# A graph network's first sweep over its edges: six one-hot columns in one VectorE instruction instead of two at a time

## The chip, the cores and the metric

The kernel runs on one core of a Trainium2 chip. The metric is the device time of one execution in microseconds, lower is better. Engines are named as the profile names them: PE (TensorE), DVE (VectorE), ACT (ScalarE), POOL (GpSimd), SP (SyncE).

## The reference

Four graph layers follow one another on 3125 nodes with 128 features, each with a residual and a layer normalisation. There are 103,125 directed edges `src -> dst`, sorted by `dst`, with a weight each. Layer 0 is dot-product attention over the edges, then a small dense network. Layer 1 has two convolutions that sum weighed neighbours. Layer 2 is three attention passes of another kind, and layer 3 a normalised convolution. Cut to what this change touches:

```
# layer 0
Q, K, V = x @ Wq + bq, x @ Wk + bk, x @ Wv + bv          # (3125, 8 heads, 16)
scores = sum(Q[dst] * K[src], -1) / sqrt(16)             # per edge and head
alpha = softmax of scores over the edges of one dst
out = segment_sum(alpha * V[src], dst) @ Wo + bo
# layers 1 and 3
agg = segment_sum(x[src] * edge_weight[:, None], dst)    # = A @ x, A[dst, src] = summed weights
```

## The kernel before

The edges are cut into steps of 128. Four steps make a group, and there are 208 groups. A function `dot_scores_and_adjacency` (L1055 on) sweeps once over all edges and does two jobs at a time, for which five engines run programs of their own, tied by counting semaphores. The loop body holds 8 groups (a ring turn, `RING_GROUPS`) and runs 26 times.

The first job is the scores of layer 0. For each step POOL gathers 128 rows of keys and values from memory into `rows` (L810, four gathers a group, one step each). ACT makes a one-hot matrix `hot_t` of the destinations from a row of local numbers (L1125 squares, L1127 clamps). PE multiplies it with the three bfloat16 parts of the queries (L1235, 12 matmuls a group, "the query matmuls"). DVE multiplies the result in PSUM by the gathered keys (`z`, L1207) and sums over each head (`logits`, L1210).

The second job builds the dense weighed adjacency matrix for layers 1 and 3, which later passes read. The edges are cut once more, into steps sorted for this job, 6 a group (`A_GROUP`). For each step DVE makes two one-hot matrices, `at_hot` (128 edges x 200, where in a span of windows the edge falls, L1183) and `lo_hot` (128 x 128, the source's low bits, L1187), and multiplies the latter by the edge weights (L1193). PE multiplies the two (L1250, with a small clearing matmul at L1247 for each pair of steps; "the adjacency matmuls"). ACT copies finished parts of PSUM to `stage` (L1166), and SP stores them in memory, a block at a time (L1107).

What sets the order around the change:

- In its loop DVE calls `make_adjacency_hots(n + 2)`, waits for the query matmuls (`asked`) and the gathered rows of group n (`landed`), and does z and logits of group n. `lo_hot` and `at_hot` have four slots (`A_HOTS`), so hots n+2 wait for the adjacency matmuls of group n-2 (`summed`).
- DVE raises `hots` behind L1187 and `weighed` behind L1193, once for each group, on the last instruction of the run. L1193 works in place and waits for `hots`.
- PE's program for group n waits for `hot_made` n, and for the logits of group n-2 (`zed`), whose PSUM bank it takes. Then come the 12 query matmuls, the waits for `hots` and `weighed` of group n, and the adjacency matmuls. In front of every second group its sequencer reads two small tables from SBUF into registers (L1227 and L797).
- ACT's program for group n begins, in every second group, with a table read (L1149) and the ask for the rows of groups n+4 and n+5 (`index_ring`, L1119), which waits for the logits of group n-3. It makes `hot_t` n+1, copies the adjacency parts of group n, waits for the rows of group n and stores their values half.
- POOL gathers as soon as the index of a pair of groups is there and the ring's place is free.

Of the kernel before, what the change touches and what calls it, by code (L numbers as in the profile page):

```python
# [22 lines left out]
ALU = mybir.AluOpType  # L23
# [4 lines left out]
P = 128  # L28
# [34 lines left out]
SPAN = BLOCKS * WIN  # L63
A_GROUP = 6
# [105 lines left out]
def over_groups(t):  # L170
    return t.rearrange("p (k d) -> p k d", d=D)
# [883 lines left out]
def dot_scores_and_adjacency(B, A, table, heads, query_parts, logits, loads):  # L1055
# [6 lines left out]
    with ExitStack() as ctx:  # L1062
# [5 lines left out]
        lo = B.sb(ctx, "lo_hot", [P, A_HOTS, A_GROUP, P])  # L1068
        at = B.sb(ctx, "at_hot", [P, A_HOTS, A_GROUP, SPAN])
# [5 lines left out]
        hots, weighed, summed, copied, room, stored = (  # L1075
            B.count("adj_" + n) for n in ("hots", "weighed", "summed", "copied", "room", "stored"))
        wait_holder = B.count("wait_holder")

        def group_rows(q, lo_col):
            return rows[:, q * GROUP * width:(q + 1) * GROUP * width].rearrange(  # L1080
                "p (k w) -> p k w", w=width)[:, :, lo_col:lo_col + D]

        def steps_of(t, n, k):
            return t[:, bass.ds(n * A_GROUP + k, 2)].rearrange("p (k o) -> p k o", o=1)

        with nc.Block() as block:
            @block.gpsimd
            def _(eng):
                with eng.Fori(0, RING_TURNS) as i:
                    for h in range(RING_GROUPS // 2):  # L1090
                        eng.wait_ge(index.sem, index.at(h + 1) + i * (RING_GROUPS // 2))
                        for q in range(2 * h, 2 * h + 2):
                            eng.wait_ge(kept[q].sem, kept[q].at(0) + i * 16)
                            eng.sem_inc(wait_holder.sem, 1)
                            for s in range(q * GROUP, (q + 1) * GROUP):
                                gather_rows(B, eng, rows, table, width, s, landed)
# [79 lines left out]
            @block.vector  # L1176
            def _(eng):
                eng.sem_inc(zed.sem, RING_GROUPS * 2)

                def make_adjacency_hots(n, slot):  # L1180
                    eng.wait_ge(summed.sem, summed.at(A_PAIRS) + n * A_PAIRS)
                    for k in range(0, A_GROUP, 2):
                        eng.tensor_tensor(at[:, slot, k:k + 2, :],  # L1183
                                          A.iota[:, :].rearrange("p (o n) -> p o n", o=1).to_broadcast([P, 2, SPAN]),
                                          steps_of(A.at, n, k).to_broadcast([P, 2, SPAN]), ALU.is_equal)
                    for k in range(0, A_GROUP, 2):
                        ins = eng.tensor_tensor(lo[:, slot, k:k + 2, :],  # L1187
                                                B.iota[:, :].rearrange("p (o n) -> p o n", o=1).to_broadcast([P, 2, P]),
                                                steps_of(A.lo, n, k).to_broadcast([P, 2, P]), ALU.is_equal)
                    ins.then_inc(hots.sem, 1)  # L1190
                    eng.wait_ge(hots.sem, hots.at(1) + n)
                    for k in range(0, A_GROUP, 2):
                        ins = eng.tensor_tensor(lo[:, slot, k:k + 2, :], lo[:, slot, k:k + 2, :],  # L1193
                                                steps_of(A.w, n, k).to_broadcast([P, 2, P]), ALU.mult)
                    ins.then_inc(weighed.sem, 1)

                for n in range(2):
                    make_adjacency_hots(n, n)
                with eng.Fori(0, RING_TURNS) as i:
                    for q in range(RING_GROUPS):  # L1200
                        n = i * RING_GROUPS + q
                        make_adjacency_hots(n + 2, (q + 2) % A_HOTS)
                        eng.wait_ge(asked.sem, asked.at(3) + n)
                        for s in range(q * GROUP, (q + 1) * GROUP):
                            eng.wait_ge(landed[s].sem, landed[s].at(16) + i * 16)
                        zz = z[:, q % 2, :]
                        eng.tensor_tensor(over_groups(zz), over_groups(B.bank(q % 2)), group_rows(q, 0), ALU.mult  # L1207
                                          ).then_inc(zed.sem, 1)
                        eng.wait_ge(zed.sem, zed.at(RING_GROUPS * 2 + 1) + n * 2)
                        eng.tensor_reduce(logits[:, bass.ds(n * (GROUP * heads), GROUP * heads)],  # L1210
                                          zz.rearrange("p (m d) -> p m d", d=dim), X_AXIS, ALU.add).then_inc(zed.sem, 1)
# [1729 lines left out]
```

## Time and the profile before

| | |
|---|---|
| median of three runs | 6320.31 us |
| the runs | 6324.8, 6320.31, 6304.53 us |
| profiled execution: time and span | 6324.8 us, 6322.7 us |
| busy share of the span: PE, DVE, ACT, POOL | 71%, 74%, 43%, 58% |
| mean granted clock of TensorE | 0.724 |
| the stage that holds the change | about 272 to 1480 us |

The profile is one execution. Times are microseconds unless marked ns. A group of instructions is a line with its engine, operation and tiles; its row gives the count, busy time, the mean of one, and the idle time of the engine just in front of them with what ended it. "Issue" is idle time that no semaphore in the profile explains. DVEq, ACTq and PEldq are the engines' sequencers. PEld is the loading of weights, which overlaps PE.

### The profile page before, as it was taken

The page shows a single profiled execution, that of the slowest core. Times are in us where ns is not written, and L with a number is a line of the kernel's source. Part 1 is how long each engine was busy: PE and PEld are TensorE (multiplying, and loading weights), DVE is VectorE, ACT ScalarE, POOL GpSimd, SP SyncE. Part 2 cuts the span into 40 slices and gives each one's busy share as a digit, 9 for nine tenths or more (in the row PEclk, how much of TensorE's full clock was granted, in tenths as well). Part 3 has the DMA queues.
Part 4 walks back from the last instruction along what each step waited for, and adds up shares of the span by engine and source line. Part 5 has one row for each costly group of instructions (what it writes and reads, how often), then busy time and mean ns, then how long its engine had stood idle before and what let it go on. Part 6 is the DMA issues. An engine that isn't in the chain of part 4 may idle for free. (4 is left out here: it accounts for less than half of the span.)

```text
span 6322.7 us, 128259 instructions
## 1 busy us (share of the span) xinstructions
PE 4480.2 (71%) x25366; PEld 3482.7 (55%) x25375; DVE 4705.6 (74%) x10133; ACT 2709.9 (43%) x6587; POOL 3669.3 (58%) x3881
## 2 busy tenths in 40 slices
PE   0578887884888896777777747777776577777746
PEld 0466666663666454556655636555555456665523
DVE  3788888887766415888888788888886988888843
ACT  0244554453554201455555525555455344554530
POOL 1476776671332001777777657777774777777710
PEclk9988888886999998565565656565656565666668
DMA  1376676674443573333333223333231233322225
GB/s 49 95 201 185 189 199 189 188 197 93 129 133 121 161 267 120 88 90 86 84 89 90 59 75 88 81 89 90 80 89 51 76 83 84 81 78 83 73 94 179
DMA packets 577604, 723.40 MB, mean 114 GB/s; under 512 B 89995, under 2 KB 424673, under 8 KB 576927
## 3 DMA queue, kind: packets, MB, share of 16 engines
q1 hardware_dynamic: 305030, 352.76, 18.4%
q0 software_dynamic: 123968, 277.70, 16.2%
q10 hardware_dynamic: 148056, 86.42, 5.1%
q8 instruction: 247, 4.05, 0.3%
q14 instruction: 303, 2.47, 0.1%
HBM read 595.96 MB, written 120.58 MB: 113 GB/s over the span
## 5 line engine op out<-in xcount | busy, mean ns | idle before, releaser
L1629 POOL DMA_INDIRECT rows<-scratch_gat,index x2496 | 2553.1, 1023 | 1324.7 <-issue 744.9
L2007 PE MATMUL sums<-mix,vhot 128*128 128x128 f32 x4992 | 1112.1, 392 | 3.1 <-issue 0.3
L810 POOL DMA_INDIRECT rows<-scratch_kv,index_ring x832 | 847.8, 1019 | 397.4 <-issue 238.0
L1952 PE MATMUL sums<-xr_part,hot_t 128*128 x7524 | 999.3, 286 | 93.0 <-DVE hot_t L1768 64.7
L2007 PEld LDWEIGHTS sums<-mix,vhot 128*128 128x128 f32 x4992 | 951.6, 284 | 50.9 <-issue 2.3
L1952 PEld LDWEIGHTS sums<-xr_part,hot_t 128*128 128x128 bf16 x7524 | 775.1, 126 | 281.1 <-issue 126.9
L1696 ACT ACTIVATE moved_sums<-sums x624 | 372.5, 597 | 1212.5 <-PE sums L2007 1104.8
L1686 ACT ACTIVATE vhot<-iota,edge_local 128x128 f32<-128x128 f32 x2496 | 789.1, 390 | 0.0
L1250 PE MATMUL sums<-at_hot,lo_hot 128*128 128x200 f32 x2496 | 668.8, 423 | 2.6
L1868 DVE TENSOR_TENSOR z<-sums,rows 128x512 f32<-128x512 f32 x624 | 426.7, 684 | 251.7 <-DMA rows<-scratch_gat,index 214.1
L1250 PEld LDWEIGHTS sums<-at_hot,lo_hot 128*128 128x128 f32 x2496 | 510.7, 236 | 61.2 <-issue 28.0
L2003 PE MATMUL sums<-zeros 128*128 128x8 bf16 x624 | 115.2, 185 | 569.4 <-ACT vhot L1690 311.6
L1854 DVE TENSOR_TENSOR mix<-rows,alpha 128x512 f32<-128x512 f32 x624 | 432.5, 694 | 69.4 <-PE sums L2007 18.9
L1876 DVE TENSOR_TENSOR z<-z,gat_a 128x512 f32<-128x512 f32 x624 | 432.7, 693 | 48.3 <-DVE carry L1813 4.3
L1690 ACT ACTIVATE vhot<-vhot,part 128x512 f32<-128x512 f32 x624 | 450.4, 722 | 20.3
L1235 PE MATMUL sums<-q_part,hot_t 128*128 x2496 | 321.9, 238 | 185.1 <-issue 125.9
L1870 DVE SCALAR_TENSOR_TENSOR z<-z 128x512 f32<-128x512 f32 x624 | 432.8, 694 | 21.5
L2003 PEld LDWEIGHTS sums<-zeros 128*128 128x128 bf16 x624 | 64.2, 103 | 698.2 <-issue 697.9
L1878 DVE TENSOR_REDUCE logits<-z 128x16 f32<-128x512 f32 (+1 forms) x624 | 428.7, 687 | 21.2
L1235 PEld LDWEIGHTS sums<-q_part,hot_t 128*128 128x128 bf16 x2496 | 227.1, 105 | 303.0 <-issue 255.3
L1166 ACT ACTIVATE stage<-sums x624 | 298.4, 498 | 171.0 <-PE sums L1250 146.3
L1183 DVE TENSOR_TENSOR at_hot<-adj_iota,adj_at 128x400 f32<-128x400 f32 x630 | 323.6, 568 | 6.5 <-PEq L1216 6.5
(510 smaller groups left out, 6585.1 us busy)
## 6 DMA issues: line engine op xcount, KB each, us to landing
piece<-scratch_adj SPq DMA_DIRECT2D x90, 1280.0 KB, 6.0
local_ring<-scratch_local_rows SPq DMA_DIRECT2D x633, 128.0 KB
scratch_spool<-rows ACTq DMA_DIRECT2D x208, 256.0 KB, 3.2
vals<-scratch_spool SPq DMA_DIRECT2D x208, 256.0 KB, 2.6
scratch_adj<-stage SPq DMA_DIRECT2D x25, 1600.0 KB
rows<-scratch_gat,index POOLq DMA_INDIRECT x2496, 2.5
local_ring<-scratch_local_rows ACTq DMA_DIRECT2D x211, 128.0 KB
mask<-scratch_masks SPq DMA_DIRECT2D x234, 80.1 KB
```

The source lines that it names most:

```text
L810: eng.indirect_dma_start(slots[:, s * width:(s + 1) * width], None, table, bass.IndirectOffsetOnAxis(ap=B.index_ring[:, s:s + 1], axis=0)) ...
L1235: ins = eng.matmul(B.ps[:, (q % 2) * 512 + k * D:(q % 2) * 512 + (k + 1) * D], hot_t[:, q % 2, k * P:(k + 1) * P], part[:, bass.ds(at_bloc ...
L1250: ins = eng.matmul(B.ps[:, bass.ds(here, SPAN)], lo[:, q % A_HOTS, k, :], at[:, q % A_HOTS, k, :], start=False, stop=True, skip_group_chec ...
L1629: eng.indirect_dma_start(rows[:, slot, q, k * D:(k + 1) * D], None, table, bass.IndirectOffsetOnAxis(ap=index[:, slot, s:s + 1], axis=0)). ...
L1686: ins = eng.activation(hot[:, v % MIXES, k * P:(k + 1) * P], B.iota[:, :], ACT.Square, scale=-1.0, bias=B.edge_local[:, bass.ds(m * GROUP ...
L1690: eng.activation(hot[:, v % MIXES, :], hot[:, v % MIXES, :], ACT.Relu, bias=B.part[:, 2:3], scale=-4.0).then_inc(hot_v.sem, 1)
L1854: eng.tensor_tensor(mix[:, v % MIXES, :].rearrange("p (k h d) -> p k h d", k=GROUP, h=heads), rows[:, of, v, :].rearrange("p (k h d) -> p ...
L1870: eng.scalar_tensor_tensor(out=zz, in0=zz, scalar=SLOPE, in1=zz, op0=ALU.mult, op1=ALU.max).then_inc(reduced.sem, 1)
L1876: eng.tensor_tensor(over_groups(zz), over_groups(zz), a, ALU.mult).then_inc(reduced.sem, 1)
L1878: eng.tensor_reduce(in_portion(lg[:, slot, 0:R], q), zz.rearrange("p (k h d) -> p k h d", k=GROUP, h=heads), X_AXIS, ALU.add).then_inc(red ...
L1952: ins = eng.matmul(B.ps[:, at + k * D:at + (k + 1) * D], hot_t[:, slot, k * P:(k + 1) * P], part[:, bass.ds(at_block, D)], start=(j == 0), ...
L2007: ins = eng.matmul(B.ps[:, bass.ds(of_block * D, D)], hot[:, v % MIXES, k * P:(k + 1) * P], mix[:, v % MIXES, k * D:(k + 1) * D], start=Fa ...
```

## The change

In `make_adjacency_hots`, each of three loops over three pairs of steps becomes one instruction over all six steps of the group. L1183 made 2 x 200 elements a partition and is now one of 6 x 200; L1187 and L1193 made 2 x 128 and are now 6 x 128. The operands are the same tensors with the same broadcasts, the semaphores are raised at the same points of the sequence, and all other programs stay as they are.

```diff
-        def steps_of(t, n, k):
-            return t[:, bass.ds(n * A_GROUP + k, 2)].rearrange("p (k o) -> p k o", o=1)
+        def steps_of(t, n):
+            return t[:, bass.ds(n * A_GROUP, A_GROUP)].rearrange("p (k o) -> p k o", o=1)
...
                 def make_adjacency_hots(n, slot):
                     eng.wait_ge(summed.sem, summed.at(A_PAIRS) + n * A_PAIRS)
-                    for k in range(0, A_GROUP, 2):
-                        eng.tensor_tensor(at[:, slot, k:k + 2, :],
-                                          A.iota[:, :].rearrange("p (o n) -> p o n", o=1).to_broadcast([P, 2, SPAN]),
-                                          steps_of(A.at, n, k).to_broadcast([P, 2, SPAN]), ALU.is_equal)
-                    for k in range(0, A_GROUP, 2):
-                        ins = eng.tensor_tensor(lo[:, slot, k:k + 2, :],
-                                                B.iota[:, :].rearrange("p (o n) -> p o n", o=1).to_broadcast([P, 2, P]),
-                                                steps_of(A.lo, n, k).to_broadcast([P, 2, P]), ALU.is_equal)
-                    ins.then_inc(hots.sem, 1)
+                    eng.tensor_tensor(at[:, slot, :, :],
+                                      A.iota[:, :].rearrange("p (o n) -> p o n", o=1).to_broadcast([P, A_GROUP, SPAN]),
+                                      steps_of(A.at, n).to_broadcast([P, A_GROUP, SPAN]), ALU.is_equal)
+                    eng.tensor_tensor(lo[:, slot, :, :],
+                                      B.iota[:, :].rearrange("p (o n) -> p o n", o=1).to_broadcast([P, A_GROUP, P]),
+                                      steps_of(A.lo, n).to_broadcast([P, A_GROUP, P]), ALU.is_equal).then_inc(hots.sem, 1)
                     eng.wait_ge(hots.sem, hots.at(1) + n)
-                    for k in range(0, A_GROUP, 2):
-                        ins = eng.tensor_tensor(lo[:, slot, k:k + 2, :], lo[:, slot, k:k + 2, :],
-                                                steps_of(A.w, n, k).to_broadcast([P, 2, P]), ALU.mult)
-                    ins.then_inc(weighed.sem, 1)
+                    eng.tensor_tensor(lo[:, slot, :, :], lo[:, slot, :, :],
+                                      steps_of(A.w, n).to_broadcast([P, A_GROUP, P]), ALU.mult).then_inc(weighed.sem, 1)
```

## Rows read from the trace of the kernel before

**Rows 1.** The page, busy time, share of the span and instructions of each engine.

```profile
PE 4480.2 (71%) x25366; PEld 3482.7 (55%) x25375; DVE 4705.6 (74%) x10133; ACT 2709.9 (43%) x6587; POOL 3669.3 (58%) x3881
```

**Rows 2.** Busy time in one stretch, the stage with the changed lines.

```profile
core 0: us, PE busy (x) PEld busy (x) DVE busy (x) ACT busy (x) POOL busy (x), PEclk, DMA share, GB/s
272.00:1480.00 1208.00, 991.81 (x5604) 794.02 (x5605) 1026.50 (x2291) 604.39 (x1140) 844.32 (x829) 0.83 0.68 190
```

**Rows 3.** DVE's groups in the stage: count, busy, mean ns, idle before.

```profile
L1183 DVE TENSOR_TENSOR at_hot<-adj_iota,adj_at 128x400 f32<-128x400 f32 x624 | 320.5, 568 | 0.0
L1193 DVE TENSOR_TENSOR lo_hot<-lo_hot,adj_w 128x256 f32<-128x256 f32 x627 | 232.5, 424 | 25.5
L1187 DVE TENSOR_TENSOR lo_hot<-iota,adj_lo 128x256 f32<-128x256 f32 x624 | 225.9, 416 | 0.0
L1207 DVE TENSOR_TENSOR z<-sums,rows 128x512 f32<-128x512 f32 x208 | 143.1, 688 | 126.2 <-PE sums L1235 116.8 <-DMA rows<-scratch_kv,index_ring 4.4 <-issue 3.4
L1210 DVE TENSOR_REDUCE logits<-z 128x512 f32 x208 | 142.7, 686 | 29.7
```

**Rows 4.** PE's groups in the stage.

```profile
L1250 PE MATMUL sums<-at_hot,lo_hot 128*128 128x200 f32 x2491 | 667.9, 423 | 2.6
L1235 PE MATMUL sums<-q_part,hot_t 128*128 x2490 | 321.0, 238 | 183.2 <-issue 125.9 <-ACT hot_t L1127 52.8 <-DVE z L1207 2.0
L1247 PE MATMUL sums<-zeros 128*128 128x8 bf16 x623 | 114.3, 183 | 30.3 <-issue 24.3 <-DVE lo_hot L1193 5.5 <-ACT stage L1166 0.2
```

**Rows 5.** POOL's group in the stage.

```profile
L810 POOL DMA_INDIRECT rows<-scratch_kv,index_ring x829 | 844.3, 1018 | 346.2 <-issue 237.4 <-ACT index_ring L1119 108.8
```

**Rows 6.** Who waited for whom in the stage: us in total, times, longest.

```profile
PE sums L1235 <- issue: 125.9, 66, 5.4
DVE z L1207 <- PE sums L1235: 116.8, 111, 4.9
PE sums L1235 <- ACT hot_t L1127: 52.8, 57, 1.6
ACT index_ring L1119 <- DVE z L1207: 45.0, 19, 3.6
```

**Rows 7.** PE's table reads in the stage: ns, least, median, most.

```profile
L1227 PEldq TENSOR_LOAD <-adj_pe_table x103: 764/1094/3308, 279.6 to 1468.6; - x103
...
L797 PEldq TENSOR_LOAD <-blocks x103: 528/544/2348, 281.0 to 1469.5; - x103
```

**Rows 8.** Timeline of DVE around 800 us: start, length.

```profile
794.07 0.69 DVE L1210 TENSOR_REDUCE logits<-z 128x512 f32 x1
...
800.23 0.69 DVE L1210 TENSOR_REDUCE logits<-z 128x512 f32 x1
800.83 1.53 DVE L1183 TENSOR_TENSOR at_hot<-adj_iota,adj_at 128x400 f32<-128x400 f32 x3
802.28 1.09 DVE L1187 TENSOR_TENSOR lo_hot<-iota,adj_lo 128x256 f32<-128x256 f32 x3
803.49 1.10 DVE L1193 TENSOR_TENSOR lo_hot<-lo_hot,adj_w 128x256 f32<-128x256 f32 x3
...
805.33 0.69 DVE L1210 TENSOR_REDUCE logits<-z 128x512 f32 x1
```

**Rows 9.** Timeline of PE in the same stretch.

```profile
802.63 1.80 PE L1235 MATMUL sums<-q_part,hot_t 128*128 x12 [0.81 <-issue]
804.65 0.18 PE L1247 MATMUL sums<-zeros 128*128 128x8 bf16 x1 [0.23 <-DVE lo_hot L1193]
```

**Rows 10.** Timeline of POOL in the same stretch.

```profile
801.41 1.28 POOL L810 DMA_INDIRECT rows<-scratch_kv,index_ring  x1 [0.30 <-issue]
803.00 1.19 POOL L810 DMA_INDIRECT rows<-scratch_kv,index_ring  x1 [0.30 <-issue]
804.49 0.94 POOL L810 DMA_INDIRECT rows<-scratch_kv,index_ring  x1 [0.30 <-issue]
```

**Rows 11.** Gathers by source line: ns, least, median, most; the stage, then the later stages.

```profile
L810 POOL DMA_INDIRECT rows<-scratch_kv,index_ring x829: 940/947/1366, 272.0 to 1461.3; - x166
...
L1629 POOL DMA_INDIRECT rows<-scratch_gat,index x2496: 940/944/1461, 2489.6 to 5992.8; - x192
```

## The prediction

> **What bounds the kernel now.** I read the page first: over the whole span DVE is the busiest engine and PE is next [rows 1]. That is an average over stages, so I then asked where the changed lines run. Lines L1183, L1187 and L1193 occur in one stage alone, from about 272 to 1480 us, and the summary of that stretch is the first thing to see: 1208 us, in which DVE is busy for 1026 us, PE for 992 and POOL for 844 [rows 2]. The stage has 208 groups, so a group takes 1208 / 208 = 5.81 us. DVE looks like the bound, at 85%. Three views say otherwise.
>
> The groups of instructions by line close the time of each engine. For DVE: 4.94 us busy a group, 0.61 us idle in front of z (126.2 us), nearly all of it ended by PE's query matmuls, and the rest semaphore gaps [rows 3]. For PE: 4.77 us busy and 213.5 us idle in front of L1235 and L1247, 1.03 us a group; together 5.80 us, the whole group [rows 4]. What ends PE's idle time is "issue" (125.9 us) and ACT's hot_t (52.8 us); DVE is named for 2.0 + 5.5 us in the whole stage [rows 4, 6]. The issue time is PE's own sequencer: once every two groups it reads two tables, with medians of 1.09 and 0.54 us, before it can issue the next query matmuls [rows 7]. So the chain that sets the pace is PE with its table reads, and at times ACT. The granted clock of this stage is 0.83, a mix of the 2.4 and the 1.2 GHz level [rows 2]; the change doesn't touch PE's work.
>
> Third, does PE ever wait for what DVE makes? The code lets DVE build hots for group n+2 in front of z of group n, and PE's query of group n needs the logits of group n-2. In the timeline the query at 802.63 could use logits made by the reduction of 794.07, over 7 us earlier, and the adjacency matmuls at 804.65 read hots finished two DVE rounds before [rows 8, 9]. The releaser "DVE lo_hot" beside the latter is the round for group n+2 that merely happened to end then. The same holds for ACT's ask, put down to z for 45.0 us [rows 6]: its semaphore value is that of the reduction of group n-3, and what delays it is its own table read.
>
> **The change, part by part.** *Fewer instructions.* Nine become three in each group. Two rows of the same form give DVE's rate: 568 ns for 400 elements and 416 ns for 256 [rows 3], 1.06 ns an element and about 0.15 us fixed. But back to back they overlap: three L1183 take 1.53 us, not 1.70, so they start (1.53 - 0.568) / 2 = 0.48 us apart, three L1187 start (1.09 - 0.416) / 2 = 0.34 us apart [rows 8]. These starts differ by 0.14 us for 144 elements, near 1 ns each, and taking 1.04 ns leaves 0.48 - 0.42 = 0.06 and 0.34 - 0.27 = 0.07 us that each instruction of a run pays besides. Six are removed: 6 x 0.07 = 0.42 us a group. From below, the saving could be nothing if six repeats streamed slower (no row shows six; with two, L1187's 416 ns are no more than L1193's 424 for as many elements); from above it is the whole fixed part, 6 x 0.15 = 0.9 us. I take 0.42, because the rows back to back are this very sequence. The new instructions should last 0.568 + 800 x 1.06 = 1.41, 0.416 + 512 x 1.06 = 0.96 and 0.42 + 0.54 = 0.96 us. Over 208 groups DVE has 87 us less to do.
>
> What is that worth? DVE's round takes 5.10 us when it waits for nothing (800.23 to 805.33) and will take 4.68 [rows 8]. The group takes 5.81 by PE. Where DVE already waits for the query, it waits 0.42 us longer: nothing. Where it runs late after a long PE step (PE's steps alternate, as the table reads fall in every second), z starts earlier, and its product is used only two or three groups later, so nothing again. The value is 0 from this side. Should the cover be gone, the price is the second rival below.
>
> *The order of signals.* hots and weighed were raised only by the third instruction of each run and now by the only one; no wait is added. At the start, hots 0 to 2 come 3 x 0.42 = 1.3 us earlier, but z of group 0 waits for its rows as well; I count 0 to 1 us gained. The last groups end in PE's matmuls and ACT's copies, so the end gains nothing.
>
> *POOL.* This is the part that may cost. The view of POOL's gathers by source line shows 940 ns at the least, 947 in the median, 1366 at the most [rows 11], with a mean of 1018 [rows 5]. The timeline tells which are stretched: the gather of 801.41 began inside the run of L1183 and took 1.28 us, that of 803.00 inside L1187's and took 1.19, that of 804.49 inside L1193's and took 0.94 [rows 8, 10]. The excess, 0.34 us in the first case, is the time to the end of the single DVE instruction that was running, and the most (1366 - 944 = 0.42 us) is about one 400-element step. In the later stages, where DVE's instructions beside the gathers have 512 elements, the most is 1461, an excess of 0.52 us [rows 11]. So the excess grows with the length of the one instruction, and it will reach 1.41 and 0.96 us where it was 0.42 and 0.3.
>
> Cost of it: a gather and the gap behind it take 0.944 + 0.30 = 1.25 us [rows 10], as long as the merged L1183 blocks, so about one gather in each group begins in it and waits 0 to 1.3 us, 0.65 in the mean; the next one then begins beyond L1187's end mostly. Now the excess is (1018 - 944) x 4 = 0.30 us a group. POOL's group goes from 4 x 1.25 + 0.30 = 5.28 to 4.98 + 0.65 = 5.63 us, at worst 4.98 + 1.3 = 6.3. POOL has 108.8 us of waits for its index in the stage, 0.52 us a group [rows 5], so 0.35 more is covered, and by the code the ask runs four groups ahead of z. At the chosen value this edit costs nothing; only over 0.8 us of excess a group, 5.81 - 4.98, does it set the pace.
>
> The Trainium skill ("SBUF — State Buffer", section "SBUF: two separate sides") states that a Vector instruction with two SBUF inputs holds a port pair that it shares with GpSimd for its whole length, so that the other waits fully. By this rule, the trace agrees for L1183 and L1187 but not for L1193, which has two SBUF inputs too and stretches no gather in the rows shown. If the merged L1193 did block, a gather would meet it with a chance of 0.96 / 1.25 and wait 0.48 us in the mean, 0.37 us more a group, and the excess would be 0.65 + 0.37 = 1.02 us instead of 0.65; that is the second price of the first rival.
>
> **Sum.** 0 (DVE's saving is covered) - 1 (start) + 0 (POOL covered) = -1 us on an execution of 6324.8 us with a span of 6322.7. That execution is the slowest of three, whose median is 6320.3; on the median the forecast is 6320 us.
>
> **Rivals.** *POOL becomes the bound (slower).* For it: only 0.17 us of cover is left by my mean (0.52 - 0.35), and in stretches such as that of 800 us a group takes 5.1 us, not 5.81 [rows 8]. Against it: the gathers have a lead to spend before z misses its rows, and z waited for rows only 4.4 us [rows 3]. If each group waits the full 1.3 us, it is (6.28 - 5.81) x 208 = +98 us, 6418; if the excess is 1.0 us a group, (5.98 - 5.81) x 208 = +35 us, 6355. It decides from 0.8 us a group.
>
> *DVE is the bound after all (faster).* For it: 85% busy, and DVE waited for PE before z in 111 of 208 groups [rows 6], so in 97 it came last. If each of those gives its 0.42 us to the end, -41 us, 6279; if all 208 do, -87 us, 6233. Against it: PE waits for no product of DVE beyond 7.5 us in all. The Trainium skill ("VectorE: DVE Perf Modes", section on the TRN2 errata) says that a fixed latency is paid by each instruction, given as 58 cycles at 0.96 GHz, and advises tiles of 512 elements or more. Estimated by that page it would be 6 x 208 x 60 ns = 75 us, if DVE set the pace.
>
> *Shifted transfers, either sign.* PE's table reads range from 0.76 to 3.3 us [rows 7]. The gathers will start at other moments, and if the mean read moved by 0.1 us, 104 pairs of groups would move the end by 10 us, inside what I call no change.
>
> **From this to the numbers.** A time within 0.3% (19 us) is about what a measurement of this kernel can't tell from none; the three runs shown spread by 0.32%. My forecast has 0.58, with 6300 to 6340 as its own range; POOL as the bound 0.20; DVE as the bound 0.15; transfers shifted beyond 0.3% 0.07, split evenly but for a little more on the faster side. So faster 0.19, same 0.58, slower 0.23. The range reaches to the partial price of each rival: 6279 below, and 6370 above, between the 35 and the 98 us.
>
> **What the changed profile would show.** The three lines 208 to 210 times each at 1.41, 0.96 and 0.96 us; DVE busy some 80 us less in the stage and its idle time in front of z, ended by PE, some 80 us more; PE's idle time in front of L1235 the same, with the same releasers; gathers of the stage up to 2.2 us at the most with a mean of 1.08 to 1.12, and POOL's waits for the index down from 109 us to some 40. The stage would still end near 1480 us. The prediction is wrong if the waits of z for gathered rows rise over some 20 us (POOL), if the idle time of PE shrinks (DVE was on the path), or if gathers stretch under the merged L1193 too, a third blocking window of 0.96 us.

## The result: slower by 1.3%, and the profile after

The changed kernel takes 6403.15 us in the median of 4 runs (6393.4 to 6404.46), against 6322.56 us before. The ratio is 1.0131 with a 95% interval of 1.0108 to 1.0152. The forecast of 6320 us was wrong, and the time lies above the range: the first rival, POOL as the bound, which had a chance of 0.20 and prices of 6355 and 6418 us, is what happened.

The summary of the stage that holds the change, by the same columns as [rows 2]; the stage now ends some 80 us later:

```profile
272.00:1560.00 1288.00, 1055.64 (x5602) 829.80 (x5601) 932.12 (x1034) 599.92 (x1138) 1036.01 (x828) 0.81 0.64 178
```

A group takes 1288 / 208 = 6.19 us instead of 5.81. DVE has 94 us less to do, POOL is busy 192 us more. The groups by line, from 272 to 1480 us, answer to [rows 3 to 5]; in the same time fewer groups are done, 194 instead of 208:

```profile
L1182 DVE TENSOR_TENSOR at_hot<-adj_iota,adj_at 128x1200 f32<-128x1200 f32 x195 | 273.2, 1401 | 1.6 <-issue 0.4
L1189 DVE TENSOR_TENSOR lo_hot<-lo_hot,adj_w 128x768 f32<-128x768 f32 x194 | 185.9, 958 | 23.9
L1185 DVE TENSOR_TENSOR lo_hot<-iota,adj_lo 128x768 f32<-128x768 f32 x194 | 184.6, 952 | 0.0
L1202 DVE TENSOR_TENSOR z<-sums,rows 128x512 f32<-128x512 f32 x194 | 133.8, 690 | 280.4 <-DMA rows<-scratch_kv,index_ring 256.4 <-PE sums L1230 23.6
```

```profile
L1230 PE MATMUL sums<-q_part,hot_t 128*128 x2334 | 323.7, 242 | 180.6 <-issue 83.8 <-ACT hot_t L1127 59.3 <-DVE logits L1205 17.8
```

```profile
L810 POOL DMA_INDIRECT rows<-scratch_kv,index_ring x778 | 972.7, 1250 | 237.1 <-issue 233.7 <-ACT index_ring L1119 3.4
```

DVE's new instructions last what was forecast, 1401, 952 and 958 ns. But z now waits 256 us for gathered rows, where it waited 4.4, and POOL hardly waits for its index any more (3.4 us, it was 108.8): POOL has become the engine that sets the pace. Its gathers last 1250 ns in the mean, not 1018, so four take 4 x (1.25 + 0.30) = 6.2 us, the length of a group. POOL's lead is gone as well: matched by their order, a z of the kernel before starts 16.3 us after the end of the last gather that it needs, in the median, and 2.8 us after it in the changed kernel. The view by source line gives the extremes, to be read beside [rows 11]:

```profile
L810 POOL DMA_INDIRECT rows<-scratch_kv,index_ring x832: 941/1004/2184, 267.6 to 1561.9; - x167
```

The timelines of DVE and of POOL over one round show where the time goes:

```profile
801.81 1.40 DVE L1182 TENSOR_TENSOR at_hot<-adj_iota,adj_at 128x1200 f32<-128x1200 f32 x1
803.12 0.95 DVE L1185 TENSOR_TENSOR lo_hot<-iota,adj_lo 128x768 f32<-128x768 f32 x1
804.20 0.96 DVE L1189 TENSOR_TENSOR lo_hot<-lo_hot,adj_w 128x768 f32<-128x768 f32 x1
806.76 0.69 DVE L1202 TENSOR_TENSOR z<-sums,rows 128x512 f32<-128x512 f32 x1 [1.60 <-DMA rows<-scratch_kv,index_ring]
807.59 0.69 DVE L1205 TENSOR_REDUCE logits<-z 128x512 f32 x1
808.19 1.40 DVE L1182 TENSOR_TENSOR at_hot<-adj_iota,adj_at 128x1200 f32<-128x1200 f32 x1
```

```profile
802.84 1.19 POOL L810 DMA_INDIRECT rows<-scratch_kv,index_ring  x1 [0.30 <-issue]
804.33 1.65 POOL L810 DMA_INDIRECT rows<-scratch_kv,index_ring  x1 [0.30 <-issue]
806.28 0.95 POOL L810 DMA_INDIRECT rows<-scratch_kv,index_ring  x1 [0.30 <-issue]
807.53 0.95 POOL L810 DMA_INDIRECT rows<-scratch_kv,index_ring  x1 [0.30 <-issue]
808.78 1.63 POOL L810 DMA_INDIRECT rows<-scratch_kv,index_ring  x1 [0.30 <-issue]
```

The gather of 802.84 began inside the merged L1182 (to 803.21) and took 0.24 us longer than a free one. The next began at 804.33, 0.13 us into the merged multiplication, and took 0.70 us longer. The one that began in z's wait and the one that began between z and the reduction took 0.95 us. The rule that fits all of them: a gather that begins inside a DVE instruction with two SBUF inputs is held until 0.12 us before that instruction's end. And the position is no accident: a gather released at the end of L1182 is followed by the next 1.25 us later, just inside L1189 (0.13 to 0.14 us after its start in every round). Counted over the records from 272 to 1480 us, 197 gathers began in L1182 and took 0.51 us longer in the mean, and 194, one in each round, began in L1189 and took 0.70 us longer. Three of the 197 were not held at all: they began within 0.03 us after the start of L1182.

### The profile page after: what moved, and what is told of

Its sections match the earlier page's. It is cut to its first block and busy times, and to the rows that moved or that the text cites. A ratio compares the mean times of both kernels' runs of the same rounds, so it can differ in the third digit from the quotient of the medians.

```text
span 6401.5 us, 125759 instructions
## 1 busy us (share of the span) xinstructions
PE 4549.2 (71%) x25374; PEld 3522.9 (55%) x25375; DVE 4617.8 (72%) x8873; ACT 2707.0 (42%) x6587; POOL 3869.9 (60%) x3881
## 5 line engine op out<-in xcount | busy, mean ns | idle before, releaser
L810 POOL DMA_INDIRECT rows<-scratch_kv,index_ring x832 | 1042.5, 1253 | 304.1 <-issue 249.9
L1245 PE MATMUL sums<-at_hot,lo_hot 128*128 128x200 f32 x2496 | 696.6, 436 | 4.4
L1863 DVE TENSOR_TENSOR z<-sums,rows 128x512 f32<-128x512 f32 x624 | 427.6, 685 | 263.6 <-DMA rows<-scratch_gat,index 218.0
L1245 PEld LDWEIGHTS sums<-at_hot,lo_hot 128*128 128x128 f32 x2496 | 530.1, 243 | 68.1 <-issue 32.2
L1230 PE MATMUL sums<-q_part,hot_t 128*128 x2496 | 346.6, 242 | 193.3 <-issue 88.6
L1202 DVE TENSOR_TENSOR z<-sums,rows 128x512 f32<-128x512 f32 x208 | 143.5, 690 | 303.1 <-DMA rows<-scratch_kv,index_ring 278.2
```

Of the source, the lines that this page charges most:

```text
L810: eng.indirect_dma_start(slots[:, s * width:(s + 1) * width], None, table, bass.IndirectOffsetOnAxis(ap=B.index_ring[:, s:s + 1], axis=0)) ...
L1230: ins = eng.matmul(B.ps[:, (q % 2) * 512 + k * D:(q % 2) * 512 + (k + 1) * D], hot_t[:, q % 2, k * P:(k + 1) * P], part[:, bass.ds(at_bloc ...
L1245: ins = eng.matmul(B.ps[:, bass.ds(here, SPAN)], lo[:, q % A_HOTS, k, :], at[:, q % A_HOTS, k, :], start=False, stop=True, skip_group_chec ...
```

## Experiments

The phase theory: POOL's gathers lock to DVE's round. What a gather costs is set by which instruction it meets, and that by the order and lengths of the instructions. Four gathers need 5.7 us of a round in the changed kernel, by hand: held in L1182, released at 1.27, at 2.53 held in L1189 to 3.2, then 4.48 and 5.73. These 5.7 us are too few, and by them alone the gathers would fit into the 5.81 us of a group: POOL took 4.98 + 1.23 = 6.2 us, as the count begins at the release in L1182 and leaves out the 0.5 us for which the gather is held there. The other times by hand in the expectations below are too low as well (with the swapped order 4.7 us, against 4.98 + 0.62 = 5.6); it is the measured excess that is compared. A first rival says that a merged instruction costs by its length, wherever it stands; a second says that the longer DVE instructions hurt PE or ACT and not POOL.

**One run merged, or two.** Each of these differs from the changed kernel in the loops alone. `{c}` is 2 (as before) or 6 (merged):

```diff
+                    for k in range(0, A_GROUP, {c}):
+                        eng.tensor_tensor(at[:, slot, k:k + {c}, :], ... steps_of(A.at, n, k, {c}) ..., ALU.is_equal)
+                    for k in range(0, A_GROUP, {c}):
+                        ins = eng.tensor_tensor(lo[:, slot, k:k + {c}, :], ... steps_of(A.lo, n, k, {c}) ..., ALU.is_equal)
...
+                    for k in range(0, A_GROUP, {c}):
+                        ins = eng.tensor_tensor(lo[:, slot, k:k + {c}, :], lo[:, slot, k:k + {c}, :], ..., ALU.mult)
```

Only `at_hot` merged: 

> Only at_hot merged. Phase theory: behind the gather held in at, the next begins at 2.53 us, at the start of the first short multiplication, held 0 or 0.3 us; four fit in 5.0 to 5.3 us; 6310 to 6335 us. Rival by length: half of the loss, 6362. Rival DVE: 6340 or more.

Only `lo_hot` merged: 

> Only lo_hot merged, once more, on a chip where the kernel before takes its usual time. Phase theory: gathers at 1.70 (held 0.59 us in the merged lo), 3.54 and 4.79; four fit in 4.8 us; 6310 to 6325 us. Rival by length: a quarter of the loss, 6342.

Only the multiplication merged: 

> Only the multiplication merged. Phase theory: gathers come at 1.70, 3.00 (held 0.49 us in the merged multiplication) and 4.75, then 6.0; four fit in 4.8 to 6.0 us by where the first begins; 6315 to 6345 us, and in the trace gathers that begin inside L1193's successor are held to 0.12 us before its end, although none was before. Rival by length: a quarter of the loss, 6342. If this line blocked nothing at any length, no gather would be held in it and the time would be 6320 or less.

`at_hot` and `lo_hot` merged, the multiplication in three: 

> at_hot and lo_hot merged, the multiplication by the weights left in three instructions. Phase theory: the gather behind the one held in at begins 2.53 us into the round, 0.14 us into the first of three short multiplications, and is held 0.16 us instead of 0.70; four gathers fit in 5.2 us instead of 5.7; 6320 to 6345 us. Rival by length (loss of 80 us shared by the squares of 1.40, 0.95 and 0.96 us): three quarters stay, 6380. Rival DVE: between, 6370 to 6400.

Measured, with the gather's mean of the stage (272 to 1470 us) and the excess it makes over 944 ns, four times a group:

| merged | time, us | ratio (95%) | gather mean, ns | excess a group, us | z waits for rows, us |
|---|---|---|---|---|---|
| none (before) | 6322 | 1 | 1018 | 0.30 | 4.4 |
| multiplication | 6331.25 | 1.0014 (0.9998 to 1.003) | 1065 | 0.48 | 10.3 |
| lo | 6324.8 | 1.0012 (1.0002 to 1.0021) | 1070 | 0.50 | 11.4 |
| at | 6332.84 | 1.0022 (1.0007 to 1.0036) | 1084 | 0.56 | 13.8 |
| at, lo | 6332.1 | 1.0021 (1.0005 to 1.0038) | 1167 | 0.89 | 110.9 |
| all | 6403.15 | 1.0131 (1.0108 to 1.0152) | 1251 | 1.23 | 253.9 |

No single run costs more than 0.22%, and the three together cost far more than the sum (0.5%). The rival by length forecast 6342 to 6380 us for these and falls. The column of z's waits tells where POOL's room ends: 4 to 14 us up to an excess of 0.56 us, 111 at 0.89 and 254 at 1.23. The time does not follow as closely: the multiplication alone and `at_hot` alone, with 0.48 and 0.56 us, were 10 and 11 us slower, as much as the kernel with 0.89. With the multiplication split, the gather behind the one held in L1183 still begins just inside it, but is held for one short instruction only. In that kernel's timelines of DVE and POOL the excess is 0.17 us where it was 0.70:

```profile
804.90 1.10 DVE L1193 TENSOR_TENSOR lo_hot<-lo_hot,adj_w 128x256 f32<-128x256 f32 x3
```

```profile
805.03 1.11 POOL L810 DMA_INDIRECT rows<-scratch_kv,index_ring  x1 [0.30 <-issue]
```

The kernel with only the multiplication merged shows that this line holds gathers, too; here one began 0.33 us into it and took 0.50 us longer:

```profile
807.66 0.96 DVE L1193 TENSOR_TENSOR lo_hot<-lo_hot,adj_w 128x768 f32<-128x768 f32 x1
```

```profile
807.99 1.44 POOL L810 DMA_INDIRECT rows<-scratch_kv,index_ring  x1 [0.30 <-issue]
```

**All merged, in another order.** The same three instructions, with `lo_hot` built first:

```diff
+                    eng.tensor_tensor(lo[:, slot, :, :], ..., ALU.is_equal).then_inc(hots.sem, 1)
                     eng.tensor_tensor(at[:, slot, :, :], ..., ALU.is_equal)
-                    eng.tensor_tensor(lo[:, slot, :, :], ..., ALU.is_equal).then_inc(hots.sem, 1)
                     eng.wait_ge(hots.sem, hots.at(1) + n)
```

> All three runs merged as in the changed kernel, with lo_hot built in front of at_hot. Phase theory (a gather that begins inside a DVE instruction with two SBUF inputs is held to about 0.12 us before its end, and the next begins 1.25 us later, so the order of the instructions decides what it meets): held in lo, a gather is released at 0.83 us of the round, the next begins at 2.08 near the end of at (0.87 to 2.19), the next at 3.4 beside z, the fourth at 4.7. Four gathers fit in a round of 4.7 us, against 5.7 us in the changed kernel; the loss goes: 6320 us, within 20. Rival by length (each merged instruction costs by its length, whatever its place): 6400, as changed. Rival DVE (longer DVE instructions hurt PE and ACT directly, not POOL): 6400.

Measured 6323.16 us, ratio 1.0001 (0.9988 to 1.0014): the whole loss is gone with every instruction as long as before the swap. The gather's mean is 1100 ns, an excess of 0.62 us a group. The timelines of DVE and POOL show the phases as forecast. Held in lo, the gather is released, the next begins near the end of at, and the one after that beside z:

```profile
803.36 0.95 DVE L1183 TENSOR_TENSOR lo_hot<-iota,adj_lo 128x768 f32<-128x768 f32 x1
804.23 1.40 DVE L1188 TENSOR_TENSOR at_hot<-adj_iota,adj_at 128x1200 f32<-128x1200 f32 x1
805.55 0.95 DVE L1193 TENSOR_TENSOR lo_hot<-lo_hot,adj_w 128x768 f32<-128x768 f32 x1
807.04 0.69 DVE L1207 TENSOR_TENSOR z<-sums,rows 128x512 f32<-128x512 f32 x1 [0.54 <-PE sums L1235]
```

```profile
803.43 1.70 POOL L810 DMA_INDIRECT rows<-scratch_kv,index_ring  x1 [0.30 <-issue]
805.43 1.01 POOL L810 DMA_INDIRECT rows<-scratch_kv,index_ring  x1 [0.30 <-issue]
806.75 0.95 POOL L810 DMA_INDIRECT rows<-scratch_kv,index_ring  x1 [0.30 <-issue]
808.00 0.94 POOL L810 DMA_INDIRECT rows<-scratch_kv,index_ring  x1 [0.30 <-issue]
```

It also prices DVE's saving: with POOL inside its room (z waits 14.2 us for rows and 231.6 us for PE), some 87 us less work on DVE are worth nothing.

**Half of the gathers.** Two kernels, the one before and the changed one, gather for every second step only, so the scores of the others are not computed; POOL clears the tile first (6.9 us). The waits of ACT and DVE for these rows go with them.

```diff
+                eng.memset(rows[:, :], 0.0).then_inc(cleared.sem, 1)
...
-                            for s in range(q * GROUP, (q + 1) * GROUP):
+                            for s in range(q * GROUP, (q + 1) * GROUP, 2):
                                 gather_rows(B, eng, rows, table, width, s, landed)
```

> The kernel before with every second gather of this stage left out, once more, beside a kernel before whose time is that of the first runs. PE theory: PE's chain with its table reads sets the pace, so the time stays within 30 us of the kernel before, plus some 8 us for the clearing of the tile at the start. Rival: if gathers or their traffic paced the stage before, 50 us less or more.

> The changed kernel with every second gather of this stage left out, once more. Phase theory: POOL needs only two gathers a round, the holds cost nothing, and the time is that of the run beside it within 10 us. Rival DVE (the longer DVE instructions hurt PE or ACT directly): it lies 80 us above the run beside it.

Measured 6304.88 us (ratio 0.9972, 0.9956 to 0.9987) and 6306.21 us (0.9982, 0.9965 to 0.9998). The second lies 1.3 us above the first, as expected: the changed kernel loses nothing when POOL has room, although its gathers are held more than ever (1346 ns in the mean, against 1029). Leaving out half of the gathers gains 14 to 18 us in the kernel before (by the medians and by the ratio), within the 30 us expected, and 7 more with the clearing counted; so the gathers were not the bound there, but not quite free either. The rival that the longer instructions hurt PE or ACT falls.

**Short instructions with one tensor.** One tensor-scalar instruction for each step, the weight applied in the same instruction (where `hots` and `weighed` are raised is cut here):

```diff
+                    for k in range(A_GROUP):
+                        eng.tensor_scalar(at[:, slot, k, :], A.iota[:, :], A.at[:, bass.ds(n * A_GROUP + k, 1)], None, ALU.is_equal)
+                    for k in range(A_GROUP):
+                        ins = eng.tensor_scalar(lo[:, slot, k, :], B.iota[:, :], A.lo[:, bass.ds(n * A_GROUP + k, 1)],
+                                                A.w[:, bass.ds(n * A_GROUP + k, 1)], ALU.is_equal, ALU.mult)
...
```

> Tensor-scalar instructions, one for each step, once more. Phase theory: holds of at most one short instruction, a gather's mean near 0.95 us. If the loop of PE and ACT sets the pace, no gain although DVE and POOL both have more room: 6320 within 20. Rival (DVE or POOL sets it): 6280 or less.

Measured 6337.59 us, ratio 1.0018 (1.0002 to 1.0035). POOL's row shows the excess nearly gone, a mean of 953 ns, and 183 us of waits for the index:

```profile
L810 POOL DMA_INDIRECT rows<-scratch_kv,index_ring x823 | 784.3, 953 | 414.7 <-issue 231.4 <-ACT index_ring L1119 183.2
```

DVE (906 us busy up to 1480 us, 1026 before) and POOL both have more room and the time does not fall: neither was the bound before. The holds are short rather than absent, and the single tensor does not keep them away. This gather began 0.10 us into the second of the `at_hot` instructions, which start 0.23 us apart and last some 0.32 us each, and it took 0.10 us longer:

```profile
294.54 1.48 DVE L1183 TENSOR_SCALAR at_hot<-adj_iota,adj_at 128x200 f32<-128x200 f32 x6
```

```profile
294.87 1.04 POOL L810 DMA_INDIRECT rows<-scratch_kv,index_ring  x1 [0.30 <-issue]
```

In the stage 210 gathers began in an `at_hot` instruction; 49 of them were held by more than 0.03 us, 0.15 us at the most, and again to some 0.12 us before its end. Under `lo_hot`, with two scalars, it was 5 of 297.

**PE's table read moved.** The block numbers of the next pair of groups are read between the query and the adjacency matmuls of the odd group, in the kernel before and in the changed one:

```diff
+                        if q % 2 == 1:
+                            blocks.read((q + 1) % RING_GROUPS, 2, n + 1)
                         eng.wait_ge(hots.sem, hots.at(1) + n)
```

> The kernel before with one of PE's two table reads (the block numbers of the next pair of groups, 0.54 us in the median) issued between the query and the adjacency matmuls of the odd group, where queued matmuls cover it. PE theory: PE's idle time in front of the query matmuls falls by 0.5 to 0.7 us a pair, up to 60 us for 104 pairs, so far as DVE's round of 5.1 and POOL's 5.3 us a group let it; 6260 to 6300 us. Rival (PE's reads are not on the path that sets the pace): 6320.

> The changed kernel with the same early table read. Phase theory: POOL, not PE, sets the pace of the changed kernel, so the read is worth next to nothing, 6390 to 6405 us. Rival (PE's chain still sets it and was only slowed): it falls as much as the kernel before does with this edit.

Both missed: 6477.56 us (ratio 1.0249, 1.0216 to 1.0282) and 6483.76 us (1.0255, 1.0221 to 1.0288). The stage now ends near 1640 us, a group takes some 6.5 us, and PE's rows of the first, from 272 to 1470 us, are to be read against [rows 4]:

```profile
L1241 PE MATMUL sums<-q_part,hot_t 128*128 x2201 | 274.7, 237 | 158.6 <-ACT hot_t L1132 143.2 <-issue 13.6
L1255 PE MATMUL sums<-zeros 128*128 128x8 bf16 x549 | 102.9, 187 | 113.6 <-issue 93.4 <-DVE lo_hot L1198 15.2 <-ACT stage L1171 4.6
```

The issue time in front of the query went, as meant (125.9 to 13.6 us), but 93 us stand in front of the adjacency matmuls instead of 24, and PE now waits 143 us for ACT's `hot_t`, where it waited 53. By the code, ACT copies a group's adjacency sums before it makes the `hot_t` after the next, so a read that delays the adjacency matmuls can come back through ACT. PE's chain alone does not explain the loss; a loop over PE and ACT would, but this is argued and not shown. One thing the pair does tell: with a group of some 6.5 us POOL has time for its holds, and the merged instructions add only 6 us.

**ACT's part of the loop shortened.** In every second group ACT makes `hot_t` of the next group first and reads its table and asks for rows afterwards; in the kernel before and in the one with the swapped order.

```diff
-                        if q % 2 == 0:
-                            ... read the table, wait for room and logits, ask(n + AHEAD, ...)
                         eng.wait_ge(off_made.sem, off_made.at(1) + n)
                         fetch(n + 3, (q + 3) % LOCALS)
                         make_hot_t(n + 1, ...)
+                        if q % 2 == 0:
+                            ... the same lines
```

> The kernel before with ACT's program reordered: in every second group it makes hot_t of the next group first and only then reads its table and asks for rows. Loop theory (the pace is set by the loop of PE's query and adjacency matmuls, ACT's copies, ACT's table read, hot_t and PE again): PE's wait for hot_t (52.8 us in the stage before) goes, 6270 to 6300 us. Rival (PE's own chain alone sets the pace, and its waits for hot_t are noise): 6320 within 10. A loss is possible if POOL's index now comes too late: PE and DVE would wait for rows.

> The same reordering of ACT with all three runs merged and lo_hot built first. If the loop of PE and ACT is shortened so far that DVE's round of 5.1 us counts, the merged instructions add to it: 10 to 30 us less than the run beside it. If PE still sets the pace alone, equal to it within 10 us.

Measured 6267.41 us, ratio 0.992 (0.9902 to 0.9939), faster than both kernels, and 6291.59 us, ratio 0.9954 (0.994 to 0.9969). PE's row of the first and POOL's and z's of the second, from 272 us:

```profile
L1235 PE MATMUL sums<-q_part,hot_t 128*128 x2495 | 313.5, 234 | 159.1 <-ACT hot_t L1127 81.6 <-issue 73.9 <-DVE logits L1210 1.2
```

```profile
L810 POOL DMA_INDIRECT rows<-scratch_kv,index_ring x830 | 918.1, 1106 | 252.9 <-issue 245.3 <-ACT index_ring L1119 7.6
L1207 DVE TENSOR_TENSOR z<-sums,rows 128x512 f32<-128x512 f32 x208 | 143.2, 688 | 225.9 <-DMA rows<-scratch_kv,index_ring 146.3 <-PE sums L1235 77.4 <-issue 1.8
```

The time is in the forecast range, but not by the reason that I gave: the wait put down to `hot_t` grew (52.8 to 81.6 us) and the issue time shrank (125.9 to 73.9). Of the 50 us, 24 are idle time of PE (183.2 to 159.1) and 25 are shorter matmuls: PE's busy time in the stage is 966 us instead of 992, at a granted clock of 0.85 instead of 0.83. With groups of 5.57 us the merged instructions do harm even in the better order: z waits 146 us for rows, and 24 us are lost against the run beside it; there a z starts 3.9 us after the end of its last gather, in the median, so POOL's lead is nearly gone again. The forecast for that one, equal or faster, missed.

**With both.** ACT's reordering and the short tensor-scalar instructions:

> ACT's reordering with the short tensor-scalar instructions, which hold no gather for long. The run with ACT's reordering alone takes 6267 us. If POOL's holds or DVE's round limit it there, this one is 10 to 40 us faster; if the loop of PE and ACT is still the bound, it lies where the fused form lay beside its kernel, 0 to 15 us above 6267.

This run, and the first ones of the kernels with `lo_hot` alone, half of the gathers and short instructions, fell on chips where the kernel before takes 8177 to 8189 us. With `lo_hot` alone merged, the stretch from 272 to 1480 us shows a granted clock of 0.71 and 140 GB/s moved there, against 0.83 and 191 GB/s in the run of the table; why stays open. There the kernel with both took 8104.8 us, ratio 0.9918 (0.9897 to 0.9939), next to the 0.992 of the reordering alone elsewhere; whether the short instructions add to it stays open. The first runs gave 0.9906 (`lo_hot` alone), 0.9382 and 0.9379 (half of the gathers, before and changed) and 0.9968 (short instructions); the two with half of the gathers agree there as well.

## Why the prediction was wrong

- *DVE's saving*: right. Durations of 1401, 952 and 958 ns against 1.41, 0.96 and 0.96 forecast, 94 us less busy time, and worth nothing, as the swapped order shows. One part of the forecast profile failed: DVE's idle time in front of z was to grow while it waited for PE, and that wait fell to 23.6 us while the one for rows grew.
- *Nothing of DVE's lies on PE's path*: right for the kernel before (the short instructions gained nothing, nor did the swapped order).
- *POOL's holds grow with the length of the instruction*: right. The most was 2184 ns, forecast 2.2 us.
- *The excess is 0.65 us a group and covered*: this is the step that failed; it was 1.23. It has two terms. Inside L1182 I took 0.65 us and it was 0.51 to 0.52. For the merged multiplication I took 0, "stretches no gather in the rows shown", and it was 0.70 us in every round. Both signs that the prediction had named for this came, z's waits for rows and gathers stretched under the merged multiplication. The row that I read was no evidence: the gather of 804.49 began when the run of L1193 from 803.49 had only 0.10 us left (803.49 + 1.10 = 804.59) [rows 8, 10], less than the 0.12 us at which a gather is free anyway. Of the 154 gathers that began under this line up to 1470 us, 150 were so, with 0.08 to 0.10 us left of the single instruction under them, placed there by the release from the instructions in front; the other 4 began within 0.03 us after an instruction's start, where one of 1.4 us holds none either. The Trainium skill ("SBUF — State Buffer", section "SBUF: two separate sides") says that a Vector instruction with two SBUF inputs keeps GpSimd out for its whole length. By this rule, the merged multiplication had to hold gathers, and the trace after agrees with 0.70 us in 194 of 194, but for the last 0.12 us of the instruction, in which a gather is free.
- *How large that would be*: I priced this case at 0.37 us more by chances, an even spread of starts. The starts are not spread, they follow a release by 1.25 us. By the threshold of the prediction (4.98 + excess over 5.81), (1.23 - 0.83) x 208 = +83 us, and the kernel lost 80.6. The 1.02 us of this case already lay beyond the threshold of 0.83 us; the forecast chose 0.65. The other runs bear the threshold out only roughly: 0.62 us cost nothing and 0.89 some 10 us, (0.89 - 0.83) x 208 = 12, but 0.48 and 0.56 us cost 10 and 11 us as well, where it gives nothing. So the match within 3 us is closer than the rule.
- *What sets the pace before*: incomplete. That neither DVE nor POOL does is shown. That PE's own chain with its table reads does is not: moving one read inside it cost 159 us instead of gaining. A loop of PE with ACT fits this, but the wait for `hot_t`, which the reordering of ACT was to remove, grew. What gives the 53 us of the reordering is not settled.

## What to carry to other kernels

Merging DVE instructions saves some 0.07 us each and lengthens the time for which each keeps POOL's gathers out, so first find out whether DVE is waited for, and how much room POOL has in a round. Before concluding from a trace that one kind of instruction does not hold another engine, look at where inside it the other's instructions begin: in a loop they are locked to each other and may never have tried the case. The order of the same instructions can be worth more than their number (here 80 us against nothing), and costs one line to try.

## What the runs showed that was not expected

The hold is a sawtooth: its length is what is left of the DVE instruction less 0.12 us (0.70 us at 0.13 us into one of 0.96; 0.17 at 0.13 into one of 0.42). z's product with one input in PSUM and the reduction held none: in the changed kernel, 75 and 133 gathers began under them and took at most 0.01 us longer. The hold works one way: 167 of the merged L1182 began beside a running gather and lasted 1.40 us, like the 39 that did not. PE's busy time is no constant of the work: the same matmuls took 992 us before, 1056 after and 966 in the fastest kernel, with granted clocks of 0.83, 0.81 and 0.85. In these three, the longer the stage took, the lower was the clock and the longer the same matmuls; which of the two leads to the other was not tested.
